# One TensorE loop for all rounds of a graph layer, passed by once empty, with the column product behind the next step's sums

## The reference, cut to what matters

```python
# x [6250,128], dst [200000] sorted, edge_attr [200000,128], all float32 but dst
agg = segment_sum(edge_attr, dst, 6250)          # 102 MB of edge rows are read
h = concat([x, agg, u[0] for every row], axis=1) # 128 + 128 + 64 columns
h = relu(h @ W1 + b1) @ W2 + b2
out = layernorm(x + h)                           # over the 128 features
```

## Time and profile before

| | |
|---|---|
| median of 3 runs | 274.97 us (274.71 to 275.29) |
| the profiled execution | 274.97 us |
| its span, first to last instruction | 273.2 us |
| TensorE busy (matmul) | 213.4 us, 78% |
| VectorE busy | 175.8 us, 64% |
| ScalarE, GpSimd busy | 50.8 us, 40.9 us |
| DMA | 110.06 MB, mean 403 GB/s |
| mean granted TensorE clock | 0.949 of full |

### The profile page before, as it was taken

How to read it: one execution, slowest core, us unless ns; L and a number is a source line. 1 busy time by engine, 2 the same in 40 slices (tenths; PEclk the granted TensorE clock), 3 DMA queues, 4 the chain that set the end, 5 groups by cost and what they waited for, 6 DMA issues and landing times.

```text
span 273.2 us, 15327 instructions
## 1 busy us (share of the span) xinstructions
PE 213.4 (78%) x6767; PEld 168.1 (62%) x6767; DVE 175.8 (64%) x435; ACT 50.8 (19%) x100; POOL 40.9 (15%) x49
## 2 busy tenths in 40 slices
PE   0886899999787886875669899876797976867872
PEld 0774687877655665644557677655476755655751
DVE  7842258698874784687434867779658576465542
ACT  0410022122211211210202322212022212121210
POOL 6400010040210210310300302102004011030020
PEclk9997579999999999999779999999799999999997
DMA  7999999999999999999999999999999999999995
GB/s 245 395 396 400 400 397 404 402 402 405 401 402 403 402 405 408 417 415 418 412 405 419 419 415 418 417 419 417 424 431 423 427 426 422 427 425 421 430 396 200
DMA packets 27327, 110.06 MB, mean 403 GB/s; under 512 B 2008, under 2 KB 3374, under 8 KB 25134
## 3 DMA queue, kind: packets, MB, share of 16 engines
q1 hardware_dynamic: 24052, 105.83, 95.7%
q10 hardware_dynamic: 3258, 4.00, 4.3%
HBM read 106.63 MB, written 3.20 MB: 402 GB/s over the span
## 4 chain that ended last, share of the span: by engine, by line
PE 60%; issue 14%; DMA 13%; DVE 9%; ACT 1%; DVEq 1%; POOL 1%; POOLq 0%
PE rows_ps L868 32%; PE cols_ps L880 15%; DMA slots<-in_edge_attr 13%; PE hid_ps L894 4%; PE hid_ps L912 3%; PE hid_ps L903 3%; PE hid_ps L888 2%; ACT rows L446 1%; DVE z L680 1%; DVE tall_ids L688 1%; DVE first_of_pair L572 1%; DVE hot L617 1%; POOL rstd L410 1%; DVE dst_local L585 1%; DVE high L699 1%
## 5 line engine op out<-in xcount | busy, mean ns | idle before, releaser
L868 PE MATMUL rows_ps<-slots,hot 64*32 64x128 f32 x6240 | 112.5, 284 | 31.7 <-issue 27.5
L868 PEld LDWEIGHTS rows_ps<-slots,hot 64*32 64x32 f32 x6240 | 93.2, 110 | 48.8 <-issue 46.4
L643 DVE TENSOR_TENSOR agg_t<-agg_t,cols_ps 128x128 f32 (+1 forms) x65 | 21.1, 324 | 83.3 <-PE cols_ps L880 81.4
L880 PE MATMUL cols_ps<-row_hot,rows 128*128 128x128 f32 (+1 forms) x260 | 55.2, 337 | 14.3 <-ACT rows L446 7.3
L617 DVE TENSOR_TENSOR hot<-edge_node,iota 128x768 f32<-128x768 f32 x65 | 61.9, 952 | 2.2 <-issue 1.9
L880 PEld LDWEIGHTS cols_ps<-row_hot,rows 128*128 128x128 f32 x260 | 40.5, 199 | 28.3 <-issue 15.1
L446 ACT ACTIVATE rows<-rows_ps 128x256 f32<-128x256 f32 x65 | 24.9, 383 | 176.7 <-PE rows_ps L868 169.6
L410 POOL TENSOR_TENSOR rstd<-var_eps,minus_half 128x4 f32<-128x4 f32 (+1 forms) x13 | 15.8, 1216 | 194.6 <-DVE var_eps L674 194.6
L633 DVE TENSOR_TENSOR row_hot<-row_node,iota 128x256 f32<-128x256 f32 (+1 forms) x65 | 37.5, 576 | 0.0
L401 POOL TENSOR_TENSOR z<-x_rows,b_all 128x512 f32<-128x512 f32 (+1 forms) x13 | 17.3, 1331 | 31.5 <-PE hid_ps L888 31.5
L680 DVE TENSOR_SCALAR z<-z,moments,rstd (+1 forms) x49 | 16.6, 398 | 1.1 <-POOL rstd L410 1.0
(11 more groups left out here) (119 smaller groups left out, 70.8 us busy)
## 6 DMA issues: line engine op xcount, KB each, us to landing
slots<-in_edge_attr SPq DMA_DIRECT2D x65, 1536.0 KB, 16.8
x_rows<-in_x ACTq DMA_DIRECT2D x11, 256.0 KB
out<-z SPq DMA_DIRECT2D x11, 256.0 KB
dst_int<-in_dst ACTq DMA_DIRECT2D x1, 384.0 KB, 4.1
dst_int<-in_dst SPq DMA_DIRECT2D x1, 384.0 KB, 4.6
x_rows<-in_x ACTq DMA_DIRECT2D x1, 192.0 KB
out<-z SPq DMA_DIRECT2D x1, 192.0 KB
rest_slot<-in_edge_attr ACTq DMA_DIRECT2D x1, 128.0 KB, 8.7
```

Source lines behind the costliest of these rows:

```text
L643: V.tensor_tensor(cols, cols, cols_ps[:, 0:n], ALU.add).then_inc(added, 1)
L868: done = T.matmul(rows_ps[i][c * SPAN:(c + 1) * SPAN, h, 0:feats], hot[j][part, c * RUN + r, :], slots[part, j, c, r * feats:(r + 1) * fea ...
L880: done = T.matmul(cols_ps[:, 0:n], rows[i][:, h, :], row_hot[j][:, h, 0:n], start=(h == 0), stop=(h == HALVES - 1))
```

## The change

PE's two loops become one body for all 13 laps, inside an outer loop of two passes. In the first pass (`real` = 0) every step is branched over and the lap loop runs once; it is made before the first ids have arrived. In the second the work is done. level2 of step t-1 now stands behind level1 of step t in all laps (for the last step of a lap it stands ahead of it), so that the very last level2 comes after the loops. All steps but that last one are 224 columns wide in `row_hot`, level2 and `add`. The spare matmul L961 goes. `turn_x`, `product1_x` and `product2` get banks of their own in PSUM and other places in the lap; `rows_ps` has two buffers instead of three.

VectorE: steps 0 to 3 unrolled, then one loop for 11 laps, shifted by one step, with the turning of the tall ids, `judge` and `make_plan` as branches in it; the last four steps and the last block are unrolled in `ending()`, which is written out twice behind a branch on `plan`. ACT: `copy_rows` in step order everywhere. SP: the last store stands inside a branch on `plan`, behind the code of the general path. The block of three pieces is now the first one instead of the last but one. GpSimd zeroes `x_rows` first, and `bias_add` runs one block further ahead.

```diff
-SETS = (0, 1, 0, 1, 2)
-DENSE_LAP = 5
-DENSE = DENSE_LAP * LAP
+SETS = (0, 1, 0, 1, 1)
+DENSE = 5 * LAP
...
 # SP
             plan_now = general_if(sp)
-            store(final)
             with sp.If(plan_now < 1):
+                store(final)
...
+            with sp.If(plan_now > 0):
+                store(final)
...
 # VectorE
+                V.tensor_tensor(row_hot[i][:, :, :],
+                                row_node[:, bass.ds(t, 1), :].rearrange("p o h -> p (o h)").unsqueeze(2).broadcast_to([P, HALVES, COLS]),
+                                iota[:, 0:COLS].unsqueeze(1).broadcast_to([P, HALVES, COLS]), ALU.is_equal).then_inc(row_hot_made, 1)
...
+            with dve.Fori(1, laps - 1) as lap:
+                one_lap(lap, counts(lap), range(-1, LAP - 1))
+            last_at = step_bases((laps - 1) * LAP - 1, LAP)
+            one_lap(laps - 1, last_at, range(-1, 0))
+
+            def ending():
+                one_lap(laps - 1, last_at, range(0, LAP - 1))
+
+                add(held, 0, DENSE_COLS)
+                residual(final, final)
+                variance(final, final)
+                normalise(final, final)
...
+            plan_now = general_if(dve)
+            with dve.If(plan_now < 1):
+                ending()
                 general()
+            with dve.If(plan_now > 0):
+                ending()
...
 # TensorE
+            def one_lap(lap, real):
                 counts(lap)
                 for j in range(LAP):
+                    with pe.If(real > 0):
+                        one_step(lap, j)
+
+            def one_step(lap, j):
+                t = lap * LAP + j
+                if j == 4:
+
+                    level2(t - 1, j - 1, COLS)
+                level1(t, lap, j)
+
+                if j == 0:
+                    with pe.If(lap > 0):
+                        level2(t - 1, LAP - 1, COLS)
+                    with pe.If(lap < 1):
+                        first_products()
+                elif j == 1:
+                    with pe.If(lap > 0):
+                        pe.wait_ge(added, lap * LAP + 1)
+                        product1_agg(lap - 1, start_of(lap - 1))
...
+                    level2(t - 1, j - 1, COLS)
+                    turn_x(lap, lap * 16 + x_landed(0, 0), True)
+                elif j == 2:
+                    with pe.If(lap > 0):
                         product2(lap - 1, lap - 1)
+                    level2(t - 1, j - 1, COLS)
+                    with pe.If(lap < final):
+                        product1_x(lap, BLOCK)
+                    with pe.If(lap > final - 1):
+                        product1_x(lap, P)
+                elif j == 3:
+                    level2(t - 1, j - 1, COLS)
...
+            with pe.Fori(0, 2) as real:
+                with pe.If(real > 0):
+                    before_laps()
+                with pe.Fori(0, real * (laps - 1) + 1) as lap:
+                    one_lap(lap, real)
+            level2(held, LAP - 1, DENSE_COLS)
             pe.wait_ge(added, steps + 1)
             product1_agg(final, start_of(final))
             product2(final, final)
```

More of the change, by code:

```diff
@@ L100, in residual_gnn_layer, with start_of, pieces_of @@
     places = blocks + 1
[L101 to L109, removed]
+    final = places - 1
+    def start_of(i):
+        return 0 if isinstance(i, int) and i == final else FIRST + (blocks - 1) * BLOCK - i * BLOCK
+    def pieces_of(i, rows, home):
+        at = start_of(i)
+        if i == 0:
+            more = at + top_rows * P
+            mid = more + top_even
+            return ((rows[at:more, :].rearrange("(p r) f -> p (r f)", r=top_rows), home(slice(0, P), 0, top_rows)),
+                    (rows[more:mid, :], home(slice(0, top_even), top_rows, ROWS)),
+                    (rows[mid:nodes, :], home(slice(top_even, top_parts), top_rows, ROWS)))
+        if i == final:
+            return ((rows[0:FIRST, :], home(slice(0, P), 0, 1)),)
+        return ((rows[at:at + BLOCK, :].rearrange("(p r) f -> p (r f)", r=ROWS), home(slice(0, P), 0, ROWS)),)
     ctx = ExitStack()
@@ L173, in residual_gnn_layer @@
         row_hot = [sb(f"row_hot{i}", [P, HALVES, COLS]) for i in range(HOTS)]
-        rows = [sb(f"rows{i}", [P, HALVES, feats]) for i in range(3)]
+        rows = [sb(f"rows{i}", [P, HALVES, feats]) for i in range(2)]
         agg_t = sb("agg_t", [P, width])
@@ L729, in counts @@
                     dve.compute_val(lap + n)
[L730 to L737, removed]
-                    t = lap * LAP + j
[L740 to L750, removed]
+                return step_bases(lap * LAP - 1, LAP)
@@ new lines, in _, with one_lap @@
+            turned_at = {-1: 0, 0: 1, 2: 2, 3: 3}
+            def one_lap(lap, at, steps_of):
+                looped = not isinstance(lap, int)
+                for j in steps_of:
+                    t = lap * LAP + j
+                    if j == 0 and looped:
+                        with dve.If(lap == JUDGE + 1):
+                            dve.wait_ge(bad_summed, 1)
+                            dve.wait_ge(level2_done, t + 1)
+                            V.tensor_copy(bad_total[:, :], bad_ps).then_inc(bad_read, 1)
+                            dve.wait_ge(bad_read, 1)
+                    add(t, at[j + 1], COLS)
+                    if j == 1:
+                        residual(lap - 1, lap - 1)
+                        if looped:
+                            with dve.If(lap == TURN + TILES):
+                                bring_tall_ids()
+                            with dve.If(lap == JUDGE):
+                                judge()
+                    elif j == 2:
+                        variance(lap - 1, lap - 1)
+                        if looped:
+                            with dve.If(lap == JUDGE + 1):
+                                make_plan()
+                    elif j == 3:
+                        normalise(lap - 1, lap - 1)
+                    if looped or j + AHEAD < LAP:
+                        make_hot(t + AHEAD, j + AHEAD)
+                    if looped and j in turned_at:
@@ L1014, in _ @@
-            pe.wait_ge(rows_made, 1)
-            for h in range(HALVES):
-                for g in range(GROUPS):
-                    part = slice(g * HALF, (g + 1) * HALF)
-                    T.matmul(row_ps[part, h, 0:tall_steps], row_src[:, 0, :, :].rearrange("p c j -> p (c j)"), ident[:, h:tall_parts:GROUPS],
-                             start=True, stop=True, tile_position=(0, g * HALF))
-                    done = T.matmul(row_ps[part, h, tall_steps:held], row_src[:, h, :, :].rearrange("p c j -> p (c j)"), ident[:, tall_parts + g::GROUPS],
-                                    start=True, stop=True, tile_position=(0, g * HALF))
```

313 lines of the change are left out of this document (110 added, 203 removed).

## The result

The changed kernel takes 282.23 us at the median of six runs (281.33 to 286.28) against 275.05 for the kernel before (274.71 to 275.62, six runs). The ratio is 1.028, with a 95% interval from 1.025 to 1.030: it is 7.2 us slower, where I had forecast 1.1 us faster. One of the six runs, 286.28, was a disturbed one and is not in the ratio. The profiled execution took 282.3 us, with a span of 280.6.

The account below looks back on a forecast made before the run. The prediction took the DMA load stream, then the tail behind the last load, as the bound. 274.97 us less 1.3 for the stream plus 0.2 for the tail gave 273.9 us, all else 0; range 272.7 to 276.4.

Parts of the forecast that it names:

- the start: Empty pass on TensorE: about four 16 KB pages at 2.4 to 3.0 us, ending at 9 to 12 us; value 0.
- The cover: Load queue at the start: five loads, over 18 us, hide level1 of step 0 being up to 5 us late.
- The gain of 1.3 in the stream: Load stream, lap of 20.7 us: 1.3 us belongs to the second loop's cold code and goes; bounds 0 to 1.3.
- The tail: After the last load: last level2 stands behind two loop ends, 0 to 0.3 us visible, 0.2 taken; rest of chain unchanged.
- rival C: Code behind the loops: a page missing in the tail adds some 2.1 us, 276.0 to 277.1 us; chance 0.15.
- the jumps of SP and VectorE: Branches past the general path near the end: a stall fits ahead of SP's last store, VectorE has time free; 0.
- Wider steps: 39 dense steps at 224 columns: 13.1 us more on PE, 9.8 on VectorE, hidden under the stream.
- rival E: TensorE, 89% busy, becomes the bound if its clock falls and the load queue runs out: 276 to 279 us; chance 0.05.
- the laps of 19.5 us between 130 and 190 us: Sign in the load stream: laps near 19.4 us between 130 and 190 us; one over 20 us would prove it wrong.
- The four packets: Sign on q8, TensorE's code queue: four or so instruction packets before 12 us, none between 20 and 260 us.
- The time from issue to landing after lap 0: Sign in the load queue: never under some 12 us after lap 0.
- the queue that runs dry: Sign against the forecast: load queue runs dry, with the DMA share under 1, pointing to TensorE as the bound.

Follow-up runs that it names:

- the late-started kernel before: Kernel before with one added wait: TensorE starts only when load 2 has landed; 278.46 and 281.65 us, ratio 1.019.
- both endings straight: Changed kernel without the empty pass, VectorE's ending and SP's last store written once, ahead of the branches on the plan; 275.13 us, ratio 1.0018.
- all repairs: Changed kernel without the empty pass, VectorE's ending and SP's last store straight, GpSimd's second memsets held until rows_made; 275.13 us, ratio 1.0011.

## Why the prediction was wrong

**The step that failed is the start.** I priced the empty pass at about four pages of 2.4 to 3.0 us each, from the idle times of the earlier trace rows. Those rows show idle time beside work, not the whole of a fetch. The distance between packets stood in the same trace, 6.2 to 7.1 us in the two cold stretches, and I did not use it; in the pass it was 6.0 us. With nothing to do meanwhile, the pass pays it in full. I also let the pass begin at 0 us; its first packet came at 5.7. Together it ended at 21.6 us instead of 9 to 12, though it waited for three pages and not four.

**The cover was overrated too.** I wrote that five loads, over 18 us of stream, stand in the queue, and took the bound of 5 us of delay as free. With the true price the delay of level1 of step 0 was 14 us. And the queue must get its next load not when it is empty but several us ahead: 6.8 us pass from issue to landing on an empty queue. Started at 9.2 us TensorE costs nothing by load 9, at 19.7 it costs 4.8, at 21.6 it costs 5.9. No rival covered this: I had a wait that is hidden as "value 0, both bounds included", and no case in which the pass itself was too long. This is why the range missed.

**The gain of 1.3 in the stream** came, with 1.1 (20.7 to 19.6 us for that lap), but its reason is not borne out: the same lap is short in the late-started kernel before, with all of the cold code.

**The tail** was right in its first part: level2 behind the two loops waits for ACT's copy 0.49 us, exactly as before, so the loop ends cost 0 and not 0.2, and no page was missing there (rival C did not happen). It was wrong in another place: level2 of step 63, moved ahead of the last level1, holds it back by 0.6 us, and the tail is 0.4 longer. I had only looked at the instruction that was moved behind the loops. The last five loads, +2.0 us, were in no step of mine; I had put the jumps of SP and VectorE at 0, each for its own wait alone. The three profiles with both endings straight give 18.8, 18.8 and 18.6 us, the seven with SP's branch 19.1 to 20.7, so the code jumps at the end are a likely part of it. The way there is not shown: a packet on q14, the other queue of instruction packets, goes by in the changed kernel's two late loads (at 261.0, 265.7 and 266.1 us), but with all repairs there are four in the last five loads and none is late.

**Wider steps** were indeed hidden at 224 columns, and the sum for TensorE was too pessimistic: level2 took 64.3 us instead of 55.2, 9.1 more and not 13.1, and level1 105.1 instead of 112.5, so that TensorE was busy 212.3 us instead of 213.4. The granted clock was 0.991 there and 0.949 before; it is not the whole reason, for with all repairs, at 0.983, TensorE was busy 218.5 us. VectorE got 15.3 us more work instead of 9.8: `row_hot` takes 802 ns on the mean instead of 673, as it is drawn out to 1.70 us in 11 of the 65 steps, each time with GpSimd's `bias_add` beside it. But rival E, which I gave 0.05, is near: another 96 columns cost 6.9 us. The price is not where I looked for it, in a queue that runs dry, but in work that is left over when the last load has landed.

Of the signs that I named, the laps of 19.5 us between 130 and 190 us came, no idle time of over 1 us inside a level1, and level2 of the last step 0.5 us behind its level1. The four packets came by 24 us and not before 12: this sign would have told the whole story. The time from issue to landing after lap 0 fell to 10.9 us (load 49), a little under the 12 that I had named. And the queue that runs dry, my sign for E, came, but not by a falling clock: TensorE started late.

## What to carry to other kernels

Price code that is met for the first time by the distance between its packets, not by the idle time that remains beside work; a pass that only touches code pays the whole distance for each page, while the same pages met during the work of lap 0 cost this stream nothing by load 9. Ask of each delay not whether the queue holds work, but whether its next entry comes while there is still more in it than one transfer takes from issue to landing. And when work is said to be hidden under a stream, look at how far the engine is behind when the stream ends, not only at whether the stream ever stops.

## What the runs showed of the hardware

- A code page of 16 KB for TensorE costs 6.0 to 6.2 us from one to the next with the load queues full, and 3.4 us with few loads. The Trainium skill, "Runtime: NRT & Kernel Launch", section "Instruction fetch mechanics", says that a taken branch to a page that is not there forces a fetch before execution goes on; the runs agree, and add the price. The section calls the crossing of a page border mostly hidden; in the kernel before such a page left TensorE up to 3.00 us of idle time.
- Once passed by, the pages stay: no idle time by issue of more than 1 us inside a level1 in the changed kernel, and no packet on q8 between 24 and 277 us.
- GpSimd's eight memsets (0.5 us each) held two small operations of VectorE for all of their 3.4 us, in three profiles. In others, with the same start times to 0.01 us, the first of them took 0.47 or 0.93 us, and 0.25 where no memset ran beside it. The Trainium skill, "SBUF — State Buffer", section "Who interferes with whom", tells of an exclusive lock on the ports that the two share, which blocks the other for the whole instruction. Here the wait was as long as eight in a row; whether it is this lock, no run shows.
